# Value tiles of a gated delta-rule layer turned through DRAM and VectorE instead of on TensorE

## What is computed

```python
mixed = xn @ W_qkv                                  # 8 key heads, 16 value heads, 128 wide each
mixed = silu(causal_conv4(mixed, conv_w))           # per channel, along the tokens
q, k, v = split(mixed)                              # q, k repeated for 2 value heads each
z = xn @ W_z;  beta = sigmoid(xn @ W_b)
g = -exp(A_log) * softplus(xn @ W_a + dt_bias)
q = l2norm(q) * 128**-0.5;  k = l2norm(k)
for t in tokens:                                    # state S is 128x128 for each value head
    S = S * exp(g[t])
    v_adj = (v[t] - k[t] @ S) * beta[t]
    S = S + outer(k[t], v_adj)
    o[t] = q[t] @ S
s = (rmsnorm(o) * norm_weight * silu(z)) @ W_out
y = two_of_eight_experts(xn)                        # 512 -> 2048 -> 512, gelu
out = x + s * silu(y)
```

## Time and profile before

| | |
|---|---|
| median of 3 runs | 2064.51 us (2063.43 to 2066.23) |
| the profiled execution's own time | 2060.95 us |
| its span in the profile | 2059.2 us |
| TensorE busy | 1997.2 us, 97% |
| VectorE busy | 1337.3 us, 65% |
| ScalarE busy | 911.0 us, 44% |
| GpSimd busy | 836.8 us, 41% |
| DMA packets | 388022, 184.25 MB; 249456 of them under 512 B |
| transfers of SyncE's queue | 37.9% of 16 engines' span |

### The profile page before, as it was taken

The page is one execution under the profiler, slowest core; times in us unless marked ns, Lnnn a source line. Parts: engine busy times, 40 slices in busy tenths (PEclk is TensorE's granted clock), DMA queues, the critical chain, the costliest instruction groups (busy, mean ns, idle before and its releaser), DMA issues.

```text
span 2059.2 us, 39550 instructions
## 1 busy us (share of the span) xinstructions
PE 1997.2 (97%) x13730; PEld 1705.4 (83%) x13730; DVE 1337.3 (65%) x3097; ACT 911.0 (44%) x2525; POOL 836.8 (41%) x2123
## 2 busy tenths in 40 slices
PE   5789999999999999999999999999999999999999
PEld 3578888888888888888888888888888888887887
DVE  6768887778787777887786445555555444447442
ACT  4465555555556565655554532222333233224221
POOL 2456576666666665757665411000111110111111
PEclk8899999999999999999999999999999999999999
DMA  4234444454336444444444223433334534303441
GB/s 131 47 74 81 102 87 96 82 94 83 93 84 106 82 98 92 86 92 84 97 80 85 84 82 72 92 78 76 83 80 84 123 82 103 72 21 123 154 149 66
DMA packets 388022, 184.25 MB, mean 89 GB/s; under 512 B 249456, under 2 KB 369136, under 8 KB 385776
## 3 DMA queue, kind: packets, MB, share of 16 engines
q1 hardware_dynamic: 354640, 177.73, 37.9%
q10 hardware_dynamic: 33184, 4.01, 1.3%
HBM read 135.26 MB, written 46.40 MB: 88 GB/s over the span
## 4 chain that ended last, share of the span: by engine, by line
PE 75%; issue 10%; DVE 6%; DMA 3%; POOL 3%; ACT 3%; SPq 1%; POOLq 0%; ACTq 0%; DVEq 0%
PE bank L333 18%; PE bank L335 18%; PE bank L334 18%; PE bank L565 3%; PE bank L574 2%; PE bank L548 2%; DMA VT<-v_dram 2%; PE bank L468 2%; PE bank L556 2%; PE bank L584 2%; PE bank L527 2%; PE bank L533 2%; POOL y_out L1825 1%; PE bank L502 1%; DVE cvx_k L1340 1%
## 5 line engine op out<-in xcount | busy, mean ns | idle before, releaser
L1771 POOL TENSOR_TENSOR prod<-A_in,V 128x60 f32<-128x60 f32 (+24 forms) x992 | 304.0, 306 | 270.6 <-DMA A_in<-a_dram 200.2
L1773 POOL TENSOR_TENSOR V<-V,prod 128x60 f32<-128x60 f32 (+24 forms) x992 | 311.6, 314 | 77.7
L1098 ACT ACTIVATE hid<-bank,bias 128x512 f32<-128x512 f32 x128 | 88.4, 691 | 455.0 <-PE bank L335 453.2
L1815 POOL TENSOR_TENSOR ffn_w_lo<-ffn_raw,ffn_w_hi 128x1024 fp32r<-128x1024 f32 x32 | 78.0, 2439 | 468.6 <-ACT ffn_w_hi L1088 464.7
L1563 DVE TENSOR_TENSOR h_lo<-hid,h_hi 128x512 fp32r<-128x512 f32 x128 | 91.1, 712 | 266.0 <-ACT h_hi L1105 266.0
L1577 DVE SCALAR_TENSOR_TENSOR gate_acc<-bank,rw,gate_acc 128x512 f32<-128x512 f32 x240 | 177.4, 749 | 58.8 <-PE bank L335 58.8
L333 PE MATMUL bank<-ffn_w_hi,h_hi 128*128 128x512 f32 x512 | 199.3, 389 | 1.3 <-DVE h_lo L1563 1.0
L333 PE MATMUL bank<-xn_hi,ffn_w_hi 128*128 128x512 f32 x512 | 200.3, 391 | 0.0
L335 PE MATMUL bank<-xn_hi,ffn_w_lo 128*128 128x512 f32 x512 | 199.3, 389 | 0.0
L334 PE MATMUL bank<-xn_lo,ffn_w_hi 128*128 128x512 f32 x512 | 199.2, 389 | 0.0
L334 PE MATMUL bank<-ffn_w_lo,h_hi 128*128 128x512 f32 x512 | 199.2, 389 | 0.0
(11 more groups left out here) (222 smaller groups left out, 5151.2 us busy)
## 6 DMA issues: line engine op xcount, KB each, us to landing
E<-eg_dram SPq DMA_DIRECT2D x64, 256.0 KB, 7.6
A_in<-a_dram SPq DMA_DIRECT2D x32, 512.0 KB, 4.0
decb<-dec_dram SPq DMA_DIRECT2D x128, 128.0 KB, 4.2
og_dram<-og SPq DMA_DIRECT2D x64, 256.0 KB, 2.2
ffn_raw<-w SPq DMA_DIRECT2D x32, 512.0 KB, 4.0
og_x<-og_dram SPq DMA_DIRECT2D x256, 64.0 KB, 2.6
ogT_dram<-og_y SPq DMA_DIRECT2D x64, 256.0 KB, 2.4
og_in<-ogT_dram SPq DMA_DIRECT2D x16, 1024.0 KB, 5.3
```

What stands on the lines that cost most here:

```text
L1098: act.activation(hid[:, i % 2, :], bank[i % 4][:, :], ACT.Gelu_apprx_tanh, bias=bias1[:, k, f * NF + ft:f * NF + ft + 1]).then_inc(S_["gel ...
L1771: pool.tensor_tensor(prod[:, 0:m, 0:n], column, V[:, vb, 0:m, j:j + 1].to_broadcast([P, m, n]), MUL).then_inc(S_["product"], 1)
L1773: pool.tensor_tensor(V[:, vb, 0:m, j + 1:B32], V[:, vb, 0:m, j + 1:B32], prod[:, 0:m, 0:n], ADD).then_inc(S_["solve_step"], 1)
L1815: pool.tensor_tensor(fw[m, "lo", n % 2][:, :], raw[:, i % 2, :], fw[m, "hi", n % 2][:, :].bitcast(f32), SUB).then_inc(S_["ffn_lo"], 1)
```

## The change

`turn_v` leaves TensorE, and its two banks are no longer used for it. Instead:
- ScalarE issues one DMA behind the Silu of v1 (`store_v`): all of `vS`, 128 partitions of 4 KB, to the new `vs_dram`.
- SyncE issues four DMAs behind its last `decb` of the step (`load_v`), one for each quarter of the partitions of the new tile `v_x`. Each brings 32 partitions x 32 pieces of 128 B, 128 KB in 1024 pieces.
- VectorE makes two transposes of 128x512 (`turn_v`, 32x32 blocks turned in place) from `v_x` to `v_tok`, behind the scans of the fourth quarter and ahead of the weight splits and of `chain_S(3)`.
- ScalarE makes the four multiplications of `put_v` within SBUF, both halves together behind `put_z32` and ahead of `mean_squares(3)`, not in the second and third quarter.
- `v_tok` has one buffer, not two; the four semaphores of `carry` become one; waits of TensorE on `v_tok` become waits on what last used the bank.

```diff
@@ tensor
             def project_v0(st):
                 if is_block(st - 1):
-                    pe.wait_ge(S_["v_tok"], 2 * st)
+                    pe.wait_ge(S_["z_gate"], CPS * (st - 1) + 3)
...
             def turn_k(st):
                 b = st - 1
-                pe.wait_ge(S_["v_tok"], 2 * b + 1)
+                if is_block(st):
+                    pe.wait_ge(S_["CP"], CPS * (st + 1))
+                else:
+                    pe.wait_ge(S_["k_rem"], b)
...
-            def turn_v(st, half):
-                b = st - 1
-                pe.wait_ge(S_["act_v0"], b + 1)
-                pe.wait_ge(S_["act_v1"], b + 1)
...
-                for i in range(2):
-                    c = 2 * half + i
-                    for h in range(REP):
-                        r = pe.transpose(TV_BANK[half][:, (REP * i + h) * P:(REP * i + h + 1) * P], vS[:, h, c * P:(c + 1) * P], C["ident"])
-                r.then_inc(S_["v_turned"], 1)
...
                     chain_state(st - 2, 1)
                     chain_out(st - 2, 1)
-                if turned:
-                    turn_v(st, 0)
...
                 if turned:
-                    turn_v(st, 1)
                     turn_k(st)
@@ scalar
             def silu(b, kind):
...
                     if b:
-                        act.wait_ge(S_["v_turned"], 2 * b)
+                        act.wait_ge(S_["v_x"], X_SET * b)
...
             def put_v(st, half):
                 b = st - 1
-                act.wait_ge(S_["v_turned"], 2 * b + half + 1)
+                act.wait_ge(S_["v_turned"], b + 1)
...
-                if b >= 2:
-                    act.wait_ge(S_["R"], CPS * (b - 1))
                 for i in range(2):
                     c = 2 * half + i
-                    r = act.mul(v_tok[:, b % 2, c, :], TV_BANK[half][:, i * REP * HD:(i + 1) * REP * HD], roots[:, b % 4, c:c + 1])
+                    r = act.mul(v_tok[:, :, c, :], v_tok[:, :, c, :], roots[:, b % 4, c:c + 1])
                 r.then_inc(S_["v_tok"], 1)
+
+            def store_v(b):
+                act.wait_ge(S_["act_v0"], b + 1)
+                act.wait_ge(S_["act_v1"], b + 1)
+                if b:
+                    act.wait_ge(S_["v_turned"], b)
+                else:
+                    act.wait_ge(S_["xT"], 14)
+                act.dma_start(vs_dram.rearrange("i b t -> b i t"), vS[:, :, :].rearrange("p h t -> p (h t)")).then_inc(S_["v_x"], 16)
...
                 if turned:
                     silu(st - 1, "v1")
+                    store_v(st - 1)
...
                     mean_squares(st - 2, 1)
-                if turned:
-                    put_v(st, 0)
...
                     put_z32(st - 1)
+                    put_v(st, 0)
+                    put_v(st, 1)
                 if chain:
                     mean_squares(st - 2, 3)
@@ vector
+            def turn_v(b):
+                dve.wait_ge(S_["v_x"], X_SET * (b + 1))
+                if b:
+                    dve.wait_ge(S_["R"], CPS * b)
+                for h in range(REP):
+                    src = v_x[:, :, :].rearrange("p (b m) j -> p m b j", b=NQD)[:, h * CPS:(h + 1) * CPS, :, :]
+                    r = dve.transpose(v_tok[:, h, :, :].rearrange("p c (b j) -> p c b j", b=NQD), src)
+                r.then_inc(S_["v_turned"], 1)
...
                 if ahead:
                     scan(st + 1, 2)
                     scan(st + 1, 3)
+                if turned:
+                    turn_v(st - 1)
                 if now and st % NSB == 2 and st // NSB + 1 < KEY_HEADS:
                     for n in range(2):
                         split_weights((st // NSB + 1) * len(PARTS) + n)
@@ sync
+            def load_v(b):
+                sp.wait_ge(S_["v_x"], X_SET * b + 16)
+                for q in range(NQD):
+                    r = slice(q * B32, (q + 1) * B32)
+                    src = vs_dram.rearrange("i b (m t) -> i (b m) t", t=P)[:, :, r]
+                    sp.dma_start(v_x[r, :, :], src).then_inc(S_["v_x"], 16)
...
                 next_decay(2)
                 next_decay(3)
+                if turned:
+                    load_v(st - 1)
```

More of the change, by code:

```diff
@@ L75 @@
 ffn_bias ffn_bias1 ffn_raw0 ffn_raw1 wo_raw og_raw0 og_raw1 og_turned0 og_turned1 og_in0 og_in1 og_in2 x_res0 x_res1 out0 out1
-rows_out eg0 eg1 dec0 dec1 begin0 begin1 a_out a_in v_out vt_in
+rows_out eg0 eg1 dec0 dec1 begin0 begin1 a_out a_in v_out vt_in v_x
 xT smallT ab_turned sums score_parts scores_sum rows_turned
-proj_k proj_q proj_v0 proj_v1 z_proj k_turned q_turned v_turned pair_kq keys queries solved state_add out_add lev_y32 lev_z32 lev_y64 lev_z64
+proj_k proj_q proj_v0 proj_v1 z_proj k_turned q_turned pair_kq keys queries solved state_add out_add lev_y32 lev_z32 lev_y64 lev_z64
 sw_hi xn_hi ab_T ab_in exp_steps exp_sum rows
-tap_k tap_q tap_v0 tap_v1 act_k act_q act_v0 act_v1 carry_k carry_q carry_v0 carry_v1 z_gate q_sq k_rem v_tok U squares y32 z32 y64 inv w_hi
+tap_k tap_q tap_v0 tap_v1 act_k act_q act_v0 act_v1 carry z_gate q_sq k_rem v_tok U squares y32 z32 y64 inv w_hi
 softplus_steps router_steps stats var shift xn xn_lo beta softplus router rows_zero
-conv_k conv_q conv_v0 conv_v1 nk nk_eps nk_beta c_neg c_rem q_eps CP E V_diag S_zero R S ms og w_lo_kq
+conv_k conv_q conv_v0 conv_v1 nk nk_eps nk_beta c_neg c_rem q_eps CP E v_turned V_diag S_zero R S ms og w_lo_kq
 half_pow rstd sw_lo k_len qd factor product solve_step w_lo_vz
@@ L191, in build @@
         Y64 = alloc(p2b, "Y64", [NCH, 2 * B32])
-        v_tok = alloc(p2b, "v_tok", [2, CPS, REP * HD])
+        v_tok = alloc(p2b, "v_tok", [REP, CPS, HD])
+        v_x = alloc(p2b, "v_x", [NQD * REP * CPS, B32])
         z_gate = alloc(p2b, "z_gate", [2, CPS, REP * HD])
@@ L249, in build @@
         KQ_BANK = (WORK_C, WORK_C)
-        TQ_BANK, TK_BANK, TV_BANK = WORK_B, WORK_C, (WORK_C, WORK_B)
+        TQ_BANK, TK_BANK = WORK_B, WORK_C
         def is_block(b):
@@ L316, in build @@
         CONV = 3
+        X_SET = 16 + 16 * NQD
         SOLVES = B32 - 1
@@ L859, in split_weights @@
                 act.copy(w_hi[kind][:, :, part * P:(part + 1) * P], w_raw[:, n % 2, :, :]).then_inc(S_["w_hi"], 1)
+            carries = 0
             def tap(b, kind):
+                nonlocal carries
+                carries += 1
                 gr, sb = b // NSB, b % NSB
@@ L867, in tap @@
                         act.wait_ge(S_[f"act_{kind}"], b)
-                    act.copy(cv[:, 0:KW - 1], C["zero"][:, 0:KW - 1]).then_inc(S_[f"carry_{kind}"], 1)
+                    act.copy(cv[:, 0:KW - 1], C["zero"][:, 0:KW - 1]).then_inc(S_["carry"], 1)
                 else:
                     act.wait_ge(S_[f"act_{kind}"], b)
-                    act.copy(cv[:, 0:KW - 1], cv[:, SB:SB + KW - 1]).then_inc(S_[f"carry_{kind}"], 1)
+                    act.copy(cv[:, 0:KW - 1], cv[:, SB:SB + KW - 1]).then_inc(S_["carry"], 1)
                 act.wait_ge(S_[f"proj_{kind}"], b + 1)
-                act.wait_ge(S_[f"carry_{kind}"], b + 1)
+                act.wait_ge(S_["carry"], carries)
                 act.mul(cv[:, KW - 1:], P_BANK[kind][:, :], taps[:, 4 * gr + n, 0:1]).then_inc(S_[f"tap_{kind}"], 1)
@@ L1046, in attention_step @@
                 if turned:
-                    put_v(st, 1)
                     put_k(st)
@@ L1190, in scalar @@
             silu(0, "v1")
+            store_v(0)
             put_z(1, 0)
@@ L1195, in scalar @@
             put_z(1, 1)
-            put_v(1, 0)
             exponents(3)
@@ L1200, in scalar @@
             put_z(1, 2)
-            put_v(1, 1)
             put_k(1)
@@ L1209, in scalar @@
             rates(3)
+            put_v(1, 0)
+            put_v(1, 1)
             for st in range(2, NU + 2):
@@ L1690, in vector @@
             gate_series(3)
+            turn_v(0)
             convolve(1, "v0")
@@ L2090, in sync @@
             load_blocks(1)
+            load_v(0)
             sp.wait_ge(S_["rows_out"], 96)
```

13 lines of the change are left out of this document (2 added, 11 removed).

## The result

The changed kernel takes **2185.6 us** (median of 4 runs, 2179.6 to 2189.8) against 2064.9 us before (4 runs beside them): ratio 1.058, 95% interval 1.055 to 1.062. The forecast was 2088, range 2065 to 2112: slower was right, but the loss is 121 us where 24 were forecast. The profiled execution has a span of 2187.6 us.

The account below looks back on a forecast made before the run. TensorE was taken to set the attention stage's pace, busy 892.56 of 900 us. Terms -13 + 2 + 9 + 4 + 3 + 16 + 3 gave +24 us on the profiled 2060.95: 2085, as median 2088, range 2065 to 2112.

Parts of the forecast that it names:

- Part 1: TensorE loses eight transposes a step; second-quarter group becomes a wait for S, third-quarter group pays: -13 us.
- Parts 2 and 3: VectorE's two added transposes (+2, and +9 in weight-splitting steps) and ScalarE's put_v before join_z64 (+4).
- Part 4: The store's issue on ScalarE ahead of chain_U(1) delays TensorE in seven steps: +3 us.
- Part 5: The store's 512 KB on the DMA engines delay VT, for which TensorE then waits: +16 us, bounds +2 and +30.
- the 17 punctual steps: Steps where VT is not late before the change, given about 1.3 us in hand and 0.25 us loss each.
- Part 6: SyncE's four loads of 4096 pieces land about when VectorE needs them, nearly all hidden: +3 us.
- rival C: Loads are late; VectorE stands at turn_v each step, others behind it: +36 us, 2124; chance 0.12.
- A: The forecast itself: VectorE's and ScalarE's fourth quarter and late VT cost over a third of the transposes' gain; chance 0.53.
- L511's wait: Sign at TensorE's first join, where it waits for VT: up from 5.5 to about 20 us.
- The sign that spoke for C: VectorE waiting for the loads at turn_v in all steps; the forecast named little wait there.
- the two kinds of steps of part 2: VectorE's transposes: 23 steps losing 0.1 us each (+2), seven weight-splitting steps losing 1.25 each (+9).
- The rule that the forecast weighed in part 5: DMA engines go round-robin between queues, so ScalarE's queue buys no lane; sum some 3 us higher.

Follow-up runs that it names:

- no_transfers: The changed kernel without the store and the four loads, VectorE transposing ScalarE's tile vS directly; 2066.1 us, ratio 1.0006 to the kernel before.
- store_only: The changed kernel with the store but without the four loads, VectorE waiting for the store's landing and then reading vS; 2123.3 us, ratio 1.0295.
- late_turn: The changed kernel with VectorE's two transposes moved behind v0's convolution and put_v to the start of the next step; 2182.0 us, ratio 1.0542.
- half_store: store_only with only v1's half of the tile stored (256 KB, pieces of 2048 B); ratio 1.0107 to the kernel before.
- direct: The changed kernel without the DRAM detour: 16 SyncE DMAs copy ScalarE's tile straight into v_x, no store; 2274.3 us, ratio 1.0989.
- loads_only: The changed kernel with the four loads each block but the store only for the first block; 2104.0 us, ratio 1.0197.

## Why the forecast was wrong, step by step

- **Part 1, TensorE's removal: right.** `keys(2)` gained nothing (a wait for S 31 times), and `keys(3)` stands right behind `turn_k`, without a wait in the step shown. Forecast -13, measured -8. Of the 5 us between, 1.9 are waits at `keys(3)` and 1.5 at the first join, which the forecast had at nothing here; the rest is within the interval.
- **Parts 2 and 3, VectorE's transposes and `put_v`: right, somewhat high.** Forecast +15, measured +9.5. The places were right: `turn_q` late 10 times (7 forecast), `join_z64` 3.6 us for 4. The prices came from rows of the same shapes: 0.69 and 0.43 us apiece in the changed kernel, 0.68 and 0.42 forecast.
- **Part 4, the store's issue: right in kind.** Forecast 3, idle of 5.4 us in 9 steps. It was 0.57 us of issuing plus the wait for the Silu right before it: U starts 0.74 us behind the Silu's end in the step shown. That the time can't be won back by moving the issue was not foreseen.
- **Part 5, the late `VT`: the right mechanism, mis-sized.** It priced 512 KB at the 381 GB/s of one us in which `A_in` moved, 1.4 us, and let `VT` slip by 1.2. The store's own pieces are as large as `A_in`'s, but it ran beside `E` and `VT` for 11 us, and `VT` slipped by 2.3. Forecast +16 with an upper bound of 30; measured 57 with part 4's. On the profiled executions TensorE's idle time grows by 33 us (30 at the first join, 5 at `state(1)`, less elsewhere) and its busy time by 25. The margin of 1.3 us that the forecast gave the 17 punctual steps was used up too: VectorE waits for `VT` 26 times and TensorE 22 times.
- **Part 6, the loads: the step that failed most, +3 for 61.** It added issue and landing times from `og_x`, read in another stretch of the run, and assumed the store landed before SyncE comes to the loads. Loads alone cost 38 us, and the wait for the landing about 23 more. This was rival C's mechanism, at 0.12 and +36, and it came on top of A and not in its place. That they were treated as alternatives kept the range below 2112.
- **The clock was missing.** The sum took each idle us at its own price. From no_transfers to after TensorE makes the same 13474 records; its idle time grows by 71 us and its busy time by 54, together the 125 us between the two profiled executions. The time at the lower level, over the whole run, grows by 108 us (31.7 to 139.9), and half of that is the 54. So the waits account for 71 us and the clock for 54; the prices of 57, 38 and 23 us above hold their share of both.

What the forecast named as signs came in part. L511's wait (now L501) went from 5.5 to 27.5 us where 20 was named; `keys(2)` waits for S; VectorE waits for `VT` in most steps (22). The sign that spoke for C, a wait for the loads, came in 28 steps where little wait was named, and `turn_q` was late 25 times, not in one step of four. TensorE's busy time was to fall by 38 us and rose by 36, from 1997.2 to 2033.1: without the transfers it did fall, by 18, and the lower clock more than took that back. No run tests the two kinds of steps of part 2 apart.

That slower came out is no luck, since the late `VT` was argued from its waits; but the parts that were right nearly cancel (-8 and +9.5), and most of the loss comes from what the forecast had at +3 or not at all.

The rule that the forecast weighed in part 5 is of the right kind: by the Trainium skill, DMA: Bandwidth & Descriptors, Issuing engines are not separate DMA queues, DMAs of ScalarE and SyncE interleave on the same 16 engines, and a second issuer saves only the time of issuing. The runs agree with it: from ScalarE the store delays `VT`, from SyncE behind `VT` it delays `decb`, and by the ratios the price over no_transfers is 60 and 78 us.

## What to carry to other kernels

A DMA share of 0.46 is not room. Before a transfer is added, take the loads that are already waited for in its stretch, give each its margin, and ask how far it slips when the new one runs beside it, not what the new one's bytes take at the best rate (here 2.3 us of slip where bytes over rate said 1.4). Beyond the margin most of the slip lands on the critical engine: of store_only's 43 us more of waiting for `VT`, TensorE lost 30. Where a store and a load of the same data follow each other, the load's issue waits for the landing, and everything behind it on that in-order queue waits too. Where TensorE sets the pace, its idle time isn't the whole price, since clock goes with it: in the runs with transfers each us of idle time over no_transfers came with 0.5 (late_turn) to some 1.2 us (half_store, direct) more of busy time, and with 0.8 in the changed kernel.

## What the runs showed of the hardware, unexpected

- One DMA of 512 KB in 4096 B pieces, issued by ScalarE alone on its queue, took 11 us from issue to landing beside SyncE's loads; it began to move 4 us after its issue (medians of 32 steps). It made `VT`, in flight beside it, 2.3 us later.
- By the ratios half the bytes cost a third of the time (21 of 60 us), and an issue some tenths of a us later did not lower it.
- 16 DMAs of 32 KB take 11.0 to 13.9 us to issue on SyncE's queue. Four of 128 KB in pieces of the same 128 B take 3.5 to 9.2 us in loads_only and 2.7 to 5.8 in the changed kernel, where SyncE has first waited for the store to land.
- TensorE's lower clock came with its waits and not with its lighter load: 0.1 us from 150 us on with eight transposes a step less and no transfers, 102.4 us with the same work and late transfers. In the changed kernel each of the 18 falls of the clock between 150 and 1310 us comes with or shortly behind a wait of TensorE, of 1.1 to 4.8 us; there are 32 waits so long, so not each brings a fall. Dead transposes that filled 8 us of the gaps left the mean granted clock of four runs at 0.970. The idle time alone doesn't fix it: late_turn idles more than the changed kernel and its clock is 0.978. What else does isn't shown.
- No run leaves out `E`'s copies, which kept all DMA engines busy at 65 GB/s in before; how much of the store's 11 us they make stays open.
